# First expert layer: where the gate product is kept and what signals it, and the order of the layer norms' root steps

## What is computed

```python
h = _layernorm(x, axis=-1) * (1 + cb) + sb
x = x + gb * _L0_ffn_ref(h, ...)          # first expert layer
...
def _L0_ffn_ref(x, ...):                   # N=1024 tokens, C=256, E=64 experts of width H=32
    su = x_flat @ w_shared_up
    y_s, g_s = jnp.split(su, 2, axis=-1)
    shared = jax.nn.silu(g_s) * y_s @ w_shared_down
    ...
    up = jnp.einsum('ecd,edh->ech', x_disp, w_up)
    g_r, v_r = jnp.split(up, 2, axis=-1)
    h_r = jax.nn.silu(g_r) * v_r
    out_r = jnp.einsum('ech,ehd->ecd', h_r, w_down)
    ...
    return (shared + routed).reshape(B, T, C)

def _layernorm(x, axis=-1, eps=1e-05):
    m = jnp.mean(x, axis=axis, keepdims=True)
    v = jnp.var(x, axis=axis, keepdims=True)
    return (x - m) / jnp.sqrt(v + eps)
```

## Time and profile before

| | |
|---|---|
| median of 3 runs | 888.38 us (887.94 to 889.82) |
| the profiled execution's own time | 887.78 us |
| its span, first to last instruction | 884.2 us |
| mean granted PE clock | 0.954 |
| busy: PE, PE weight load | 784.5 us (89%), 639.0 (72%) |
| busy: DVE, ACT, POOL | 556.6 us (63%), 454.0 (51%), 250.6 (28%) |
| HBM traffic | 62 GB/s over the span |

### The profile page before, as it was taken

One profiled execution on the slowest core, in us unless ns is written; L12 is line 12 of the kernel. 1 busy time (PEld: TensorE's weight loads), 2 busy tenths in 40 slices (PEclk: granted clock), 3 DMA queues, 4 the chain that ended last, 5 costly groups with the idle time before them and its releaser, 6 DMA issues.

```text
span 884.2 us, 13454 instructions
## 1 busy us (share of the span) xinstructions
PE 784.5 (89%) x4594; PEld 639.0 (72%) x4594; DVE 556.6 (63%) x1284; ACT 454.0 (51%) x982; POOL 250.6 (28%) x181
## 2 busy tenths in 40 slices
PE   6887999989999899999899989999995429999991
PEld 5766788877888778988788878888884325666661
DVE  6667758677686776777768667898795651122113
ACT  3565747757566576576667436646433203323320
POOL 1005201044010160110511326666761012333310
PEclk9898999999999999999999999999997658999996
DMA  6010000010000100000200045556635501111104
GB/s 261 1 37 1 1 1 1 14 48 1 1 1 1 60 3 1 1 1 1 82 1 1 19 131 192 177 154 201 183 107 214 214 15 35 46 43 45 47 7 142
DMA packets 22274, 55.08 MB, mean 62 GB/s; under 512 B 2909, under 2 KB 8414, under 8 KB 21056
## 3 DMA queue, kind: packets, MB, share of 16 engines
q1 hardware_dynamic: 17728, 46.75, 15.5%
q0 software_dynamic: 2208, 5.12, 2.0%
q10 hardware_dynamic: 2272, 2.36, 0.8%
HBM read 49.76 MB, written 5.37 MB: 62 GB/s over the span
## 4 chain that ended last, share of the span: by engine, by line
PE 70%; DVE 16%; ACT 5%; DMA 4%; issue 3%; POOL 0%; SPq 0%; DVEq 0%; ACTq 0%; POOLq 0%
PE ps L1419 15%; PE ps L1420 14%; PE ps L1421 14%; PE ps L1797 9%; PE ps L1524 5%; PE ps L1815 5%; DVE mx L1000 3%; DVE pT_lo L1014 2%; DMA wbc<-combine 2%; PE ps L1664 1%; DVE o_f L1102 1%; PE ps L1807 1%; PE ps L1651 1%; DMA wqkv_raw<-in_w_attn 1%; DVE fc L1183 1%
## 5 line engine op out<-in xcount | busy, mean ns | idle before, releaser
L692 ACT ACTIVATE prob<-ps,negb,rqs 128x128 f32<-128x128 f32 (+7 forms) x128 | 106.7, 834 | 73.5 <-DVE negb L1005 72.7
L490 POOL TENSOR_TENSOR oT_lo<-o_f,oT_hi 128x512 fp32r<-128x512 f32 x32 | 41.9, 1308 | 281.0 <-ACT oT_hi L771 281.0
L681 ACT ACTIVATE pT_hi<-ps 128x512 fp32r<-128x512 f32 (+1 forms) x192 | 88.7, 491 | 62.4 <-PE ps L1524 56.4
L1000 DVE TENSOR_REDUCE mx<-ps 128x1 f32<-128x128 f32 (+7 forms) x128 | 96.4, 753 | 24.2 <-PE ps L1516 22.7
L1014 DVE TENSOR_TENSOR pT_lo<-ps,pT_hi 128x512 fp32r<-128x512 f32 (+1 forms) x192 | 99.8, 547 | 2.4 <-ACT pT_hi L681 2.2
L1797 PE MATMUL ps<-wgu,xgT 128*128 x184 | 88.5, 605 | 1.0 <-ACT xgT L844 1.0
L1524 PE MATMUL ps<-ident,prob 128*128 128x128 f32 x576 | 86.4, 276 | 0.9 <-DVE qT_lo L1036 0.6
L1419 PE MATMUL ps<-pT_hi,v_hi 128*128 128x512 f32 x192 | 73.6, 383 | 15.1 <-DVE pT_lo L1014 15.1
L516 POOL TENSOR_TENSOR w_sp<-w_raw,w_sp 128x768 fp32r<-128x768 f32 x34 | 68.2, 2007 | 47.1 <-ACT w_sp L666 47.1
L1419 PE MATMUL ps<-kT_hi,qT_hi 128*128 128x512 f32 (+1 forms) x192 | 70.4, 367 | 5.5 <-ACT prob L692 3.7
L1398 DVE TENSOR_TENSOR hid<-fa,ps 128x512 f32<-128x512 f32 x23 | 15.8, 687 | 93.0 <-PE ps L1797 93.0
(11 more groups left out here) (250 smaller groups left out, 2014.9 us busy)
## 6 DMA issues: line engine op xcount, KB each, us to landing
w_raw<-in_ffn SPq DMA_DIRECT2D x34, 384.0 KB, 6.5
wbc<-combine SPq DMA_DIRECT2D x32, 256.0 KB
wgu<-in_gate_up SPq DMA_DIRECT2D x8, 1024.0 KB, 12.0
wdn<-in_down SPq DMA_DIRECT2D x8, 512.0 KB, 10.4
wqkv_raw<-in_w_attn SPq DMA_DIRECT2D x4, 768.0 KB, 4.2
wo_raw<-in_w_out SPq DMA_DIRECT2D x4, 512.0 KB, 3.2
wmod_t<-in_wmod SPq DMA_DIRECT2D x1, 1536.0 KB, 14.2
x<-in_x ACTq DMA_DIRECT2D x2, 512.0 KB, 7.0
```

What stands on the lines that cost most here:

```text
L490: nc.gpsimd.tensor_tensor(oT_lo[:, m % HPG, :], o_f[:], oT_hi[:, m % HPG, :], ALU.subtract).then_inc(oT_lo_done, 1)
L681: nc.scalar.activation(pT_hi[:, unit % NUNITS, 0:nb, qi * P:(qi + 1) * P], ps[:, ROTATING[place % 3], 0:nb * P].rearrange("p (j t) -> p j ...
L692: nc.scalar.activation(prob[:, n % 3, 0:w], ps[:, pair:pair + 2, :].rearrange("p b k -> p (b k)")[:, 0:w], ACT.Exp, bias=negb[:, n % 2:n % ...
L1000: nc.vector.reduce_max(mx[:, i:i + 1], ps[:, pair:pair + 2, :].rearrange("p b k -> p (b k)")[:, 0:w], AX.X).then_inc(row_max, 1)
```

## The change

In the first expert layer DVE writes the first product back into the value bank of PSUM instead of into `fb`, and the second product reads it there; in units 0 and 17 one product writes `fc` directly and the copy is gone. `up` signals after its gate half (`gate_up_done`) and again after its value half (`up_done`); the silu waits for the first, the product for silu and the second. `up(u)` waits for `silu_done(u-2)` before its gate half and for `weighted(u-2)` before its value half, in place of `gated(u-2)` before both; the silu waits for `weighted(u-2)` in place of `gated(u-2)`. `gated` now counts only routed units. The place of `fb` stays reserved.

The roots of the layer norms take one third-order step of four instructions and one Newton step of three, with the constants scaled so that the first step's result is 8/3 of the root. Where they were split over two units, the third-order step comes first and the Newton step second. The q/k norms stay as they were.

```diff
--- before.py
+++ after.py
@@ -279,9 +279,9 @@
         wT = keep("wT", [E0, 512])
-        w_sp, wbc, _, fa, fb, fc, hid_hi, hid_lo = stage(
+        w_sp, wbc, _, fa, _, fc, hid_hi, hid_lo = stage(
             ("w_sp", [P, NW, 2, 6 * P], F32R), ("wbc", [P, NC0, 512], F32), ("apart", [P, 8 * 256], F32),
-            ("fa", [P, 2, 512], F32), ("fb", [P, 2, 512], F32), ("fc", [P, 2, 512], F32),
+            ("fa", [P, 2, 512], F32), ("beside_fa", [P, 2, 512], F32), ("fc", [P, 2, 512], F32),
             ("hid_hi", [P, 2, 512], F32R), ("hid_lo", [P, 2, 512], F32R))
@@ -358,6 +358,7 @@
         x_in_sum = sem("x_in_sum")
+        gate_up_done = sem("gate_up_done")
         c_loaded = sem("c_loaded")
@@ -771,9 +772,9 @@
             def gate_half(u):
-                act.wait_ge(up_done, u + 1)
+                act.wait_ge(gate_up_done, u + 1)
                 if u >= 2:
-                    act.wait_ge(gated, u - 1)
+                    act.wait_ge(weighted, u - 1)
                 nc.scalar.activation(fa[:, u % 2, :], ps[:, UPS[u % 2], :], ACT.Silu).then_inc(silu_done, 1)
@@ -879,11 +880,18 @@
 
-            def root_step(s, link_):
-                v, y, t = rs_in[:, s], rs_y[:, s], rs_t[:, s]
-                link_(nc.vector.tensor_tensor(t, y, y, ALU.mult))
-                link_(nc.vector.scalar_tensor_tensor(t, t, -0.5, v, ALU.mult, ALU.mult))
-                link_(nc.vector.scalar_tensor_tensor(y, t, 1.5, y, ALU.add, ALU.mult))
+            def cubic_step(tiles):
+                v, y, t = (r[:, roots_of(tiles)] for r in (rs_in, rs_y, rs_t))
+                link(nc.vector.tensor_tensor(t, y, y, ALU.mult))
+                link(nc.vector.tensor_tensor(t, t, v, ALU.mult))
+                link(nc.vector.scalar_tensor_tensor(t, t, -10.0 / 3.0, t, ALU.add, ALU.mult))
+                link(nc.vector.scalar_tensor_tensor(y, t, 5.0, y, ALU.add, ALU.mult))
+
+            def newton_step(tiles):
+                v, y, t = (r[:, roots_of(tiles)] for r in (rs_in, rs_y, rs_t))
+                link(nc.vector.tensor_tensor(t, y, y, ALU.mult))
+                link(nc.vector.scalar_tensor_tensor(t, t, -27.0 / 1024.0, v, ALU.mult, ALU.mult))
+                link(nc.vector.scalar_tensor_tensor(y, t, 9.0 / 16.0, y, ALU.add, ALU.mult))
 
@@ -905,9 +913,9 @@
 
-            def root_steps(tiles, k):
-                for _ in range(k):
-                    root_step(roots_of(tiles), link)
+            def root_steps(tiles):
+                cubic_step(tiles)
+                newton_step(tiles)
 
@@ -951,7 +959,7 @@
             variances(tiles_of(0))
-            root_steps(tiles_of(0), NEWTON)
+            root_steps(tiles_of(0))
             normalise(lambda t: x[:, t, :], xn_a, tiles_of(0))
@@ -960,7 +968,7 @@
             variances(tiles_of(1))
-            root_steps(tiles_of(1), NEWTON)
+            root_steps(tiles_of(1))
             normalise(lambda t: x[:, t, :], xn_a, tiles_of(1))
@@ -1162,25 +1170,26 @@
                 if n == 123:
-                    root_steps(tiles_of(0), 2)
+                    cubic_step(tiles_of(0))
                 if n == 124:
-                    root_steps(tiles_of(0), 1)
+                    newton_step(tiles_of(0))
                     shifts(tiles_of(0))
...
             def gate(u):
+                value = ps[:, UPS[u % 2] + 1, :]
                 dve.wait_ge(silu_done, u + 1)
-                nc.vector.tensor_tensor(fb[:, u % 2, :], fa[:, u % 2, :], ps[:, UPS[u % 2] + 1, :],
-                                        ALU.mult).then_inc(gated, 1)
-                dve.wait_ge(gated, u + 1)
+                dve.wait_ge(up_done, u + 1)
                 if u >= 2:
...
                 if i == 0:
-                    nc.vector.tensor_copy(fc[:, u % 2, :], fb[:, u % 2, :]).then_inc(weighted, 1)
+                    nc.vector.tensor_tensor(fc[:, u % 2, :], fa[:, u % 2, :], value, ALU.mult).then_inc(weighted, 1)
                 else:
                     k = IT0 * h + i - 1
+                    nc.vector.tensor_tensor(value, fa[:, u % 2, :], value, ALU.mult).then_inc(gated, 1)
+                    dve.wait_ge(gated, k + 1)
                     dve.wait_ge(wbc_in[k % NC0], 16 * (k // NC0) + 16)
-                    nc.vector.tensor_tensor(fc[:, u % 2, :], fb[:, u % 2, :], wbc[:, k % NC0, :],
+                    nc.vector.tensor_tensor(fc[:, u % 2, :], value, wbc[:, k % NC0, :],
                                             ALU.mult).then_inc(weighted, 1)
@@ -1236,9 +1245,9 @@
                     variances(tiles_of(1))
-                    root_steps(tiles_of(1), 1)
+                    cubic_step(tiles_of(1))
                 if u == 2:
-                    root_steps(tiles_of(1), 2)
+                    newton_step(tiles_of(1))
                     shifts(tiles_of(1))
@@ -1293,7 +1302,7 @@
             variances(range(NT))
-            root_steps(range(NT), 3)
+            root_steps(range(NT))
             shifts(range(NT))
@@ -1301,12 +1310,12 @@
             variances(tiles_of(1))
-            root_steps(tiles_of(1), 3)
+            root_steps(tiles_of(1))
             state_weighted(1)
...
             variances(tiles_of(1))
-            root_steps(tiles_of(1), 3)
+            root_steps(tiles_of(1))
             shifts(tiles_of(1))
@@ -1584,14 +1593,16 @@
                 if u >= 2:
-                    pe.wait_ge(gated, u - 1)
+                    pe.wait_ge(silu_done, u - 1)
                 tok = slice(512 * h, 512 * h + 512)
                 for v in range(2):
+                    if v and u >= 2:
+                        pe.wait_ge(weighted, u - 1)
                     for kc in range(KC):
...
                                     hT_hi[:, kc, tok], hT_lo[:, kc, tok], kc == 0, kc == KC - 1)
-                ins.then_inc(up_done, 1)
+                    ins.then_inc(up_done if v else gate_up_done, 1)
```

## The result

| | before | after |
|---|---|---|
| median of 4 runs of each | 888.64 us (887.94 to 889.82) | 883.75 us (883.52 to 884.85) |
| ratio, with its 95% interval | | 0.9949 (0.9934 to 0.9964) |
| profiled execution's own time | 887.78 us | 884.85 us |
| its span, mean granted clock | 884.2 us, 0.954 | 883.0 us, 0.953 |
| DVE busy | 556.6 us | 527.2 us |

What follows compares the result with a forecast made beforehand. PE's matmul spacing was taken to bound the first expert layer, DVE's slowness mattering only at PE's gaps. Layer 3.45 plus roots 1.6 gave 5.05 us off 887.78, so 882.7, or 883.3 for the median; range 881.7 to 886.5.

Steps and rivals of the forecast that it cites:

- (a): Early in the first expert layer, 533.32 to 533.59 us, PE late as POOL waited behind a slowed `fc`; 0.25 us gained.
- (b): PE's late starts at 575 and 578 us, from late `w_sp` and `hid_lo`, vanish with two restarts; 0.8 us gained.
- (c): At 614.52 us PE waits 0.79 us for `xn_h`; only DVE's share of it, 0.5 us, comes back.
- (d): Layer's end: last `up` to last `down` shrinks from 4.73 to 2.95 us as DVE catches up; 1.8 us gained.
- (e): Smaller spots in the first expert layer where PE gets time back; 0.1 us in all.
- more comes back: Rival at 882.1 us: stall (c) goes whole, with its restart and small gaps, 1.2 us more; chance 0.13.
- Roots: Layer-norm root chains of 7 instructions for 9, each 0.40 us shorter: 1.2 us after the layer, 0.4 in attention, sum 1.6.
- The half signal: Silu may start 1.4 us before `up` ends: worth nothing in mid-layer, 0.6 us at the last unit.
- The new wait: Value half of `up` waits for `weighted(u-2)`, hence `wbc`; costs nothing until landings pass 13.3 us after issue.
- One of the prediction's signs of being wrong: In the expert layer, PE idle before a third group of six matmuls with DVE `fc` as releaser.
- the price of the rival: Rival "slower", 891 us: `wbc` landings beyond 13.3 us cost each unit the excess in full, about +3; chance 0.05.
- The start of the first expert layer unmoved but for 0.4 us: Sign of being right: the layer's start shifts only by the 0.4 us of the attention root chain.

Runs made afterwards that it cites:

- e2: After with the three Newton steps of before, so the expert-layer edit alone; 883.58 us, ratio 0.9950 to before.
- e3: After, but the silu waits for all 12 matmuls of its unit instead of the first 6; 885.34 us, ratio 0.9971 to before.
- e6: After with the new root steps in the q/k norms of attention too; 881.49 us, ratio 0.9926 to before.
- e1: Before with the new root steps alone, expert layer unchanged; 885.86 us, ratio 0.9969 to before.
- e4: After with the first product in SBUF as before, keeping the split signal and new root steps; 885.77 us, ratio 0.9966 to before.
- e12: As e4, but from unit 29 on the silu waits for the whole unit; one run, 886.34 us.
- e10: After with each `wbc` load issued a whole unit later, after the `down` that follows; one run, 888.39 us.

## Why the prediction was right

**What bounds the kernel.** Right: PE's spacing is unchanged, and all of the layer's gain stands at the four places where its starts had lain further apart. Over the whole kernel DVE has 29.4 us less to do; the layer is 3.4 us shorter.

**The terms of the layer.**

| place | predicted | measured |
|---|---|---|
| (a) up to `down(3)` | 0.25 | 0.30 |
| (b) 575 and 578 | 0.8 | 0.82 |
| (c) at `xn_h` | 0.5 | 0.69 |
| (d) the end | 1.8 | 1.61 |
| (e) smaller spots | 0.1 | none seen |
| sum | 3.45 | 3.42 |

The sum is nearer than its terms, of which two miss by 0.2 in opposite directions. (a) holds a gain and a loss: e2, with the old root steps, gained 0.46 there, and after 0.16 less by its longer root chain in unit 1, a loss that the prediction took as 0 out of 0 to 0.2. (c) gave more than the forecast: PE was 0.96 us late there by the spacing, and 0.27 are left; (d) is short by 0.17 since 3.12 us and not 2.95 lie between `up` and `down`: the product begins 0.25 us after the last matmul's end as its spacing gives it, for which I had allowed a hand-over of 0.04. In e2, e3 and e6 stall (c) is gone whole: the `fc` that starts its path, released by a landing, lies 83.21 to 83.27 us behind the first weighted product there, and 83.74 in after. So the last 0.27 us depend on half a microsecond in one landing, and the rival "more comes back" came true there in part.

**A reading of the earlier trace rows.** The prediction has the 691 ns rows of `fc` where POOL is idle. Of the nine such rows in before that holds for three. The other six began 0.05 to 0.06 us ahead of POOL's `w_sp`, and it was POOL that took longer, 2.34 to 2.35 us for its 1.83 (before, POOL and DVE):

```profile
559.25 2.35 POOL L516 TENSOR_TENSOR w_sp<-w_raw,w_sp 128x768 fp32r<-128x768 f32 x1 [2.78 <-ACT w_sp L666]
...
559.19 0.69 DVE L1183 TENSOR_TENSOR fc<-fb,wbc 128x512 f32<-128x512 f32 x1
```

In each of the 23 slow rows a POOL instruction had started first. At 590.95 us, for one, `fc` began 0.06 us behind a `w_sp` and took 2.34 us. So in these rows the one that starts first isn't held up, and the other is; 0.06 us either way decided over 1.65 us on DVE (before, POOL and DVE):

```profile
590.89 1.85 POOL L516 TENSOR_TENSOR w_sp<-w_raw,w_sp 128x768 fp32r<-128x768 f32 x1 [1.36 <-ACT w_sp L666]
...
590.95 2.34 DVE L1183 TENSOR_TENSOR fc<-fb,wbc 128x512 f32<-128x512 f32 x1
```

**Roots.** Predicted 1.2 in the tail and 0.4 in attention. Measured in attention 0.39; in the tail 0.73 in the pair of profiles, 1.1 from before to e1, 1.2 from e2 to after. Six small instructions fewer at 0.20 us make the 1.2. All traces together say the same: the tail is 32.52 to 32.98 us in the three kernels with the old steps and 31.10 to 31.79 in the eleven with the new ones, 1.3 between the means. The rows on DVE show the seven, 0.20 apart (first and last):

```profile
675.22 0.17 DVE L885 TENSOR_TENSOR rs_t<-rs_y 128x8 f32<-128x8 f32 x1
...
676.42 0.17 DVE L894 SCALAR_TENSOR_TENSOR rs_y<-rs_t,rs_y 128x8 f32<-128x8 f32 x1
```

**Costs.** 0.69 us was taken for both products; they take 0.689 and 0.692. The Trainium skill ("VectorE: DVE Perf Modes", section "The TRN2 errata") would have made `fc` some 65 ns longer for its PSUM source, an estimate from that page; with 692 ns beside 691 for the undisturbed row with two SBUF inputs, the trace doesn't agree for this shape. The Trainium skill ("SBUF — State Buffer", section "Who interferes with whom") has GpSimd and a two-SBUF-input VectorE instruction exclude each other. The runs agree: of the two kernels with the early signal, e4 with both inputs in SBUF has a median of 1626 ns and after, with one in PSUM, 692, POOL's work being the same.

**The half signal: one step failed.** "Worth nothing in the middle, 0.6 at the last unit" is right for after (e3: 0.57). As a statement on the edit it is wrong: alone it gives 1.24 us at the end (e4), 0.87 of it from the silus of units 29 to 33 (e12), for it also lets DVE catch up: the last `fb` starts 0.62 us behind `up` and not 1.86. I had counted the silu's 7 waits for PE and not asked where they lie. The sum didn't suffer, because (d) was worked out for both edits at once, as a new path and not as two savings.

**The new wait.** It was costed at nothing up to landings of 13.3 us; it cost nothing. One of the prediction's signs of being wrong, PE idle with `fc` as releaser, did show, once, at unit 3, and it is neutral there, since `down(1)` waits for the same product. The reason given for the middle of the layer was right and the price of the rival wrong: "each unit pays the excess in full" would have made e10 38 us slower, and the milder working in its expectation, also from a fixed landing, 13. e10's layer grew by 5.0, at another wait, and that of before by 2.8. The step that failed there took 10.45 and 12.7 us as the transfer's own duration, when part of it goes away with a later issue, 2 us at unit 16 and 3.3 in the median.

**"The start of the first expert layer unmoved but for 0.4 us"** couldn't be read from the two profiles: it moved by 3.44 us the other way with the granted clock. Between executions with the same clock up to 100 us (before, 524.38, and e1, 523.42) it moved by 1.0, of which 0.7 lie between the 31st score maximum and the last. In after the same stretch was 340.63 us long, at a clock of 0.98 from 200 to 300 us.

## What to carry to other kernels

Where one engine has no gaps in its pattern, don't count what another engine saves: list the places where the pattern breaks, go back from each to what is late there, and cost only the share that the edit shortens; the sum of four such places came out right to 0.1 us, single places to 0.2, while DVE's saving in the whole kernel was nine times as large. For two edits that meet on one path, work out the new path once and not each saving by itself. And the time from a transfer's issue to its landing isn't a constant to be added to a new point of issue: in this kernel a delay of 2.3 us didn't move a landing, and moving the issue ahead of another load pushed back the load that mattered more.

## What the runs showed of the hardware

- Where the clock falls is different from execution to execution of the same program: the two profiles of after begin the layer at 527.82 and 526.78 us, at a clock of 0.98 up to 508 us; those of e1 and e6, at 0.99, begin it at 523.42 and 522.76. Runs of before on one chip lay between 885.3 and 891.7 us; of the 35 beside e1 to e4, those with a mean granted clock of 0.957 or more (7 runs) had a mean span of 884.4 us, those below 0.953 (17 runs) 886.8, and the 11 in between 884.8. A difference of 1 us in such a kernel is to be looked for in distances inside a trace.
- A DVE product of 128x512 from SBUF and PSUM into PSUM takes 689 ns, into SBUF 680.
- Where `fc` with two SBUF inputs and a POOL instruction overlap, the later of the two is held up, in all 23 slow rows and in six of the nine fast ones of before: `fc` up to 2337 ns for 691, `w_sp` 2.35 us for 1.83, and POOL's scaling of `w_raw` had a median of 1180 ns beside the slow products of before and 742 in after.
- Small DVE instructions are held up too: the step `rs_t<-rs_t,rs_in` on 128x4 takes 0.16 us in the quiet rows, and beside POOL's work in after it took up to 0.72:

```profile
612.31 0.74 POOL L511 TENSOR_TENSOR w_raw<-w_raw,gates 128x256 f32<-128x256 f32 x1 [0.64 <-DMA w_raw<-in_ffn]
612.35 0.72 DVE L893 SCALAR_TENSOR_TENSOR rs_t<-rs_t,rs_in 128x4 f32<-128x4 f32 x1
```
